# Expert products of a fused attention and mixture-of-experts layer: scaled and summed on VectorE from PSUM, with the clipping of all heads on GpSimd

## What is computed

```python
exp_x = jnp.exp(jnp.clip(x - x_max, -50.0, 50.0))      # first ("plain") attention, all 16 heads
...
h = _swiglu(flat @ W1_shared)                          # one hidden layer shared by the 8 experts
for e in range(E):                                     # E = 8; w is zero except for two experts a token
    routed = routed + h @ W2_experts[e] * w[:, e:e + 1]
out = x + (shared + routed)
return _rmsnorm(out, norm2_w)
```

## Time and profile before

| what | value |
| --- | --- |
| median of 3 runs | 1968.94 us (1968.68 to 1974.44) |
| profiled execution: its time, its span | 1971.31 us, 1969.5 us |
| mean granted TensorE clock | 0.979 of full speed |
| PE busy | 1798.6 us (91%) |
| DVE busy | 1633.5 us (83%) |
| ACT busy | 1446.3 us (73%) |
| POOL busy | 1180.6 us (60%) |

### The profile page before, as it was taken

One profiled execution on the slowest core, in us unless ns is written; L12 is line 12 of the kernel. 1 busy time (PEld: TensorE's weight loads), 2 busy tenths in 40 slices (PEclk: granted clock), 3 DMA queues, 4 the chain that ended last, 5 costly groups with the idle time before them and its releaser, 6 DMA issues.

```text
span 1969.5 us, 33956 instructions
## 1 busy us (share of the span) xinstructions
PE 1798.6 (91%) x10244; PEld 526.8 (27%) x10244; DVE 1633.5 (83%) x2741; ACT 1446.3 (73%) x3095; POOL 1180.6 (60%) x1759
## 2 busy tenths in 40 slices
PE   5888899999999999999999999999999999999964
PEld 1122222222222232222222232222222222222222
DVE  4999998979899898989889898989989898987110
ACT  1378777778787788788777788777778887877622
POOL 3344548466674847567584856657485666738244
PEclk9899999999999999999999999999999999999977
DMA  4122222212122221212222121212222121220100
GB/s 123 31 64 73 72 70 59 76 56 84 57 63 76 60 80 56 84 57 71 70 58 81 57 81 57 82 57 59 81 61 78 56 85 57 62 69 28 45 25 6
DMA packets 120255, 126.34 MB, mean 64 GB/s; under 512 B 35196, under 2 KB 86780, under 8 KB 119932
## 3 DMA queue, kind: packets, MB, share of 16 engines
q1 hardware_dynamic: 119112, 123.39, 21.0%
q10 hardware_dynamic: 960, 0.79, 0.2%
HBM read 29.11 MB, written 22.02 MB: 26 GB/s over the span
## 4 chain that ended last, share of the span: by engine, by line
PE 55%; DVE 27%; SPq 7%; issue 4%; DMA 3%; ACT 3%; POOL 1%; POOLq 0%; ACTq 0%; DVEq 0%
DVE negmax L857 18%; PE score_ps L550 15%; PE o_ps L585 13%; PE side_ps L657 13%; SPq L394 6%; PE side_ps L644 4%; DVE weights L865 2%; PE side_ps L626 2%; PE side_ps L630 2%; PE side_ps L614 1%; DMA res_old<-res_new 1%; PE shift_ps L565 1%; PE side_ps L649 1%; DVE hidden L902 1%; PE side_ps L600 1%
## 5 line engine op out<-in xcount | busy, mean ns | idle before, releaser
L857 DVE TENSOR_REDUCE negmax<-score_ps 128x1 f32<-128x512 f32 x2048 | 1293.5, 681 | 167.5 <-PE score_ps L550 160.2
L693 ACT ACTIVATE weights<-shift_ps 128x512 f32<-128x512 f32 x2048 | 1114.2, 604 | 273.6 <-PE shift_ps L565 249.6
L550 PE MATMUL score_ps<-kt,qt 48*128 48x512 bf16 x2048 | 670.0, 394 | 74.6 <-DVE negmax L857 55.7
L565 PE MATMUL shift_ps<-qt,kt 51*128 51x512 bf16 x2048 | 655.8, 387 | 8.5 <-DMA qt<-max_rows 5.3
L585 PE MATMUL o_ps<-weights,vt 128*32 128x512 f32 x4096 | 551.4, 611 | 0.4 <-POOL weights L1048 0.4
L1048 POOL TENSOR_SCALAR weights<-weights 128x2048 f32<-128x2048 f32 x192 | 366.0, 1906 | 207.6 <-ACT weights L693 189.6
L550 PEld LDWEIGHTS score_ps<-kt,qt 48*128 48x128 bf16 x2048 | 148.7, 94 | 850.0 <-DVE negmax L857 746.8
L657 PE MATMUL side_ps<-w_sb,hidden 128*128 128x512 f32 x512 | 255.7, 622 | 18.6 <-ACT spread L727 14.0
L727 ACT ACTIVATE spread<-side_ps,gate 128x128 f32<-128x128 f32 x512 | 159.5, 372 | 134.2 <-PE side_ps L657 132.4
L644 PE MATMUL side_ps<-x1T,w_up_sb 128*128 128x512 f32 x256 | 151.7, 676 | 16.0 <-DVE hidden L902 8.6
L565 PEld LDWEIGHTS shift_ps<-qt,kt 51*128 51x128 bf16 x2048 | 150.3, 94 | 43.3 <-ACT weights L693 30.8
(11 more groups left out here) (108 smaller groups left out, 1407.5 us busy)
## 6 DMA issues: line engine op xcount, KB each, us to landing
qt<-q_parts SPq DMA_DIRECT2D x768, 32.0 KB
kt<-k_parts SPq DMA_DIRECT2D x744, 32.0 KB
o_rows<-o_sb SPq DMA_DIRECT2D x64, 256.0 KB, 2.0
swung<-turned SPq DMA_DIRECT2D x64, 128.0 KB, 2.4
heads_raw<-o_rows SPq DMA_DIRECT2D x64, 128.0 KB
inv_wide<-inv_rows SPq DMA_DIRECT2D x32, 256.0 KB, 3.3
x_in<-in_x_dram SPq DMA_DIRECT2D x16, 256.0 KB, 3.5
xn_mid<-xn_new SPq DMA_DIRECT2D x16, 256.0 KB, 3.4
```

Of the source, the lines that this page charges most:

```text
L550: pe.matmul(score_ps[:, score_bank(a, t), :], qt[a][row:row + HROWS, slot, 128 * tile:128 * tile + 128], kt[a][row:row + HROWS, slot, :], ...
L565: pe.matmul(shift_ps[:, shift_bank(a, t), :], kt[a][row:row + HROWS + MROWS, slot, 128 * tile:128 * tile + 128], qt[a][row:row + HROWS + M ...
L693: act.activation(weights[:, i % 8, tile, :], shift_ps[:, shift_bank(a, t), :], ACT.Exp, scale=SCALE).then_inc(weighed, 1)
L857: dve.tensor_reduce(negmax[:, i // 8, tile, i % 8:i % 8 + 1], score_ps[:, score_bank(a, t), :], AX.X, ALU.max, negate=True).then_inc(max_t ...
```

## The change

- ACT's `weight_experts` (32 scaled copies of 128 x 128 in an iteration) and POOL's `mix` (24 additions) go, with their three buffers.
- DVE gets a `mix` of its own. In quarter t of exp n and again in quarter t + 1 it does two instructions on 128 x 128 that read a product from PSUM and the gate as a per-row scalar: one multiplies and adds into `out_sb`, the other into a second sum `others` (which the first product of a tile writes with a plain multiplication). The second pair waits on the semaphore of the first and frees the bank.
- POOL's new `join` adds `others` to `out_sb` at the start of the next even step (128 x 512), in front of `square_out`.
- POOL clips all 16 heads; DVE's eight half-head clips go. Head 15 is clipped first thing in the next even step. PE waits for POOL's clip alone.
- POOL's lists are reordered: `root` before the first `rope_less_first`, `finish` behind the first part of `router`, `divide` of the rotary attention between clips 6 and 7 (before: behind clip 8), `third` behind clips 4 and 5.
- Eight entries of AT move: z 28 to 26 (ACT), shares 36 to 34 and square_x1 47 to 45 (DVE), act_v 1 to 0, act_q_plain_2 3 to 4; dve_exp is new, act_exp and act_exp_gap go.

```diff
-      "copy0": 52, "z": 28, "shares": 36, "top": 27, "square_x1": 47,
+      "copy0": 52, "z": 26, "shares": 34, "top": 27, "square_x1": 45,
...
-                        pe.wait_ge(clip_pool, cnt(b, lag, 12, 3 * quad + 3))
-                        pe.wait_ge(clip_dve, cnt(b, lag, 8, 2 * quad + 2))
+                        pe.wait_ge(clip_pool, cnt(b, lag, 16, 4 * quad + 4))
...
+            def mix(b, n, half):
+                if not live(b, -2):
+                    return
+                tile, e = n // 2, 2 * half
+                if half == 0:
+                    full(dve, b, f"exp{n}")
+                    if n == 0:
+                        dve.wait_ge(route, cnt(b, -2, ROUTE_A + ROUTE_B, ROUTE_A + ROUTE_B))
+                        need(dve, joined, cnt(b, -2, 1, 0))
+                        taken(dve, b, "shared_out")
+                    else:
+                        taken(dve, b, f"exp{n - 1}")
+                else:
+                    dve.wait_ge(mixed, cnt(b, -2, 8, n + 1))
...
+                dve.scalar_tensor_tensor(out=out_sb[:, tile, :], in0=product(0), scalar=share_of(0),
+                                         in1=out_sb[:, tile, :], op0=ALU.mult, op1=ALU.add)
+                if n % 2 == 0 and half == 0:
+                    last = dve.tensor_scalar(others[:, tile, :], product(1), share_of(1), None, ALU.mult)
+                else:
+                    last = dve.scalar_tensor_tensor(out=others[:, tile, :], in0=product(1), scalar=share_of(1),
+                                                    in1=others[:, tile, :], op0=ALU.mult, op1=ALU.add)
+                last.then_inc(mixed if half == 0 else free(f"exp{n}"), 1)
...
+            def join(b):
+                if live(b, -3):
+                    taken(pool, b + (-1), "exp7")
+                    pool.tensor_tensor(out_sb[:], out_sb[:], others[:], ALU.add).then_inc(joined, 1)
+                    pool.wait_ge(joined, cnt(b, -3, 1, 1))
...
             def even(b):
+                clip(b + (-1), 15)
                 split_max(b, "max_rope1")
                 square_out(b)
                 turn(b, 0)
                 turn(b, 1)
+                root(b, -3, 1)
                 rope_less_first(b, 0, q_rest, q_parts)
-                root(b, -3, 1)
                 rope_less_first(b, 1, k_rest, k_parts)
+                router(b, True)
                 finish(b)
-                router(b, True)
...
             def square_out(b):
                 if live(b, -3):
+                    join(b)
                     pool.tensor_tensor(square, out_sb[:], out_sb[:], ALU.mult).then_inc(squared, 1)
...
             def odd(b):
                 clip(b, 0)
                 split_max(b, "max_plain1")
                 clip(b, 1)
                 clip(b, 2)
-                mix(b, 0)
+                clip(b, 3)
+                clip(b, 4)
                 third(b, 1, PLAIN, 0, q_rest, q_parts)
+                clip(b, 5)
                 third(b, 1, PLAIN, 1, k_rest, k_parts)
-                mix(b, 1)
...
                 clip(b, 6)
+                divide(b, ROPE)
+                clip(b, 7)
                 clip(b, 8)
-                divide(b, ROPE)
+                clip(b, 9)
                 split_max(b, "max_rope0")
-                mix(b, 5)
                 square_x1(b)
-                clip(b, 9)
+                clip(b, 10)
                 place_v(b, ROPE)
                 root(b, -1, 0)
-                clip(b, 10)
-                mix(b, 6)
+                clip(b, 11)
+                clip(b, 12)
                 norm_weight(b, x1, 0, -1, x1_done)
-                mix(b, 7)
-                clip(b, 12)
                 clip(b, 13)
                 clip(b, 14)
```

## The result

The changed kernel takes **1939.48 us** (median of four runs, 1936.54 to 1945.56) against 1969.36 before: ratio 0.985, 95% interval 0.982 to 0.988. Measured again beside later runs it took 1943.26 (six runs), ratio 0.987, 0.985 to 0.989. The profiled execution is the longest of the first four, 1945.56 us with a span of 1943.7. PE is busy 93% of it, DVE 84%, ACT 68% and POOL 55%.

The account below looks back on a forecast made before the run. PE bounds the odd step's exp0 to exp6, DVE its last 15.60 us. 1971.3 - 25 - 4 - 3 + 2 = 1941.3, less 2.4 for the median: 1939 us; range 1925 to 1964, the forecast's own 1928 to 1948 (chance 0.62).

Parts of the forecast that it names:

- The main term: End of the odd step: DVE loses head 11's half clips, gains exp7's pairs; net 1.8 us a step, 25 in 14.
- What was to be late next: End of odd step: DVE waits some 0.4 us for quarter 54's score, then k_rope reads hold PE about a microsecond.
- The price of a pair: Two new DVE instructions on 128 x 128 from PSUM: 0.28 us alone, 0.48 a pair; upper end 0.74.
- the cover of 0.2: Behind exp0 to exp6: DVE's pair, maximum and pair take 1.66 us of PE's 1.86 other work, leaving 0.2; cost nothing.
- Rival B: New DVE instructions cost ACT's 372 ns, 0.74 a pair; PE loses 1.15 us a step; 1964 us total; chance 0.13.
- rival C: DVE's mixes wait for POOL's clips as its half clips did: 9 us a step, about 2065 us total; chance 0.09.
- The first batches: Batches 0 and 1 have no experts, so clips go without replacement: 4 us gained in batch 0, 0 in batch 1.
- place (1): POOL's odd step: division now before clip 7, which may reach PE late; 0 to 0.6 us a step, 2 in all.
- The end: After the last scores: exps 0.1 us nearer, 1.6 in all, plus about 1 at ACT's scaling of x; together 3.
- the way of x1: At the end, ACT's copies no longer stand before its scaling of x: 0 to 1.1 us gained, say 1.
- Places (2) and (3): POOL's clip 15 and join before the square DVE sums; `finish` and `third` behind the router's step: both costed at 0.
- Rival A: POOL's new order gives half the gain back, 0.6 and 0.4 us a step, 14 in all: 1953 us; chance 0.16.

Follow-up runs that it names:

- Experiment 8: Changed kernel with the division behind clip 8 and exp7's product handled as before (ACT copies, POOL adds behind clip 14): 1945.17 us, ratio 0.988.
- Experiments 1 to 4: Kernel before, POOL clipping all heads: 2029.01 us; changed kernel, DVE half clips kept: 1967.39; kernel before, head 11's clip to POOL: 1980.55; first without POOL's additions: 1944.86.
- experiment 5: Changed kernel with POOL's clip 9 back behind the square of x1 and clip 10 behind the root: 1952.16 us, ratio 0.990.
- experiment 9: Changed kernel with the constant 0.25 in place of the gate's per-row scalar in all 32 scaled sums of a batch: 1931.82 us, ratio 0.980.
- experiment 10: Changed kernel with a third DVE instruction in each pair, writing a product times its gate to an unread tile: 2001.68 us, ratio 1.015.
- Experiment 6: Kernel before with POOL's twelve clips a batch left out, DVE's half clips and POOL's additions kept: 1943.41 us, ratio 0.987.
- experiments 7, 11 and 12: Changed kernel with the division behind clip 8: 1940.00 us; with z, shares, v and q_plain's second part at old quarters: 1940.97; repeated unchanged: 1943.26.
- experiment 3: Kernel before with only head 11's clip moved from DVE to POOL, ahead of its mix 6: 1980.55 us, ratio 1.005.

## Why the prediction was right

**The time and the step that gives it.** 1939 us were predicted and 1939.48 measured. That they agree so closely is luck: the same kernel took 1943.26 in its second measurement, and several smaller terms were wrong, as told below. The main term is not luck. The end of the odd step was to give 1.8 us in each of 14 steps, and gave 1.72 from quarter 47 to 63 in most steps and 1.7 to 1.9 in undisturbed iterations. What was to be late next was late next: 0.30 of DVE for a score where 0.4 was put, then PE at the reads of k_rope, 0.82 and 0.21. PE's idle time in the second part fell from 3.1 to 1.41, where about 1.5 was put. Experiment 8 shows that the waits at k_rope are the limit: with less work for DVE ahead of them, they stay as long.

**What the argument left out.** It priced DVE's side of the exchange and took POOL's room as a matter of order. Experiments 1 to 4 show that it is the condition: in the last 15.60 us of the odd step before, DVE was busy 15.51 and POOL 14.43, and of the second number the prediction made no use. A clip given to POOL comes back as a wait for POOL unless POOL loses its additions; the mixes on DVE bring nothing unless the half clips go. The halves alone are worth +60 and -2 us (the second within the noise), both together -24 to -30. It also missed that clips 9 and 10 get better places (experiment 5).

**The price of a pair.** It took 0.48 from a statistic without a per-row scalar; 0.60 from start to end and 0.52 along the chain were measured, and experiment 9 puts the difference on the scalar. From the cycles in the Trainium skill, "VectorE: DVE Perf Modes", the section on the TRN2 errata, the prediction had estimated 0.52 a pair, and left it; the chain has 0.52. Behind exp0 to exp6 the size mattered little, since 0.09 us of the cover of 0.2 was left. At the end of the odd step and in the tail it did matter: the cheaper pairs of experiment 9 are worth 8 to 11 us in all. Rival B's mechanism is real, though: experiment 10 takes 0.52 more behind each exp and is 60 us slower. B failed on its price, 0.74 a pair: a DVE instruction lasts almost ACT's 372 ns, but the next begins 0.26 us after its start.

**No wait for POOL's clips (rival C).** The spread of 339 to 352 ns in the tile gate, with 156 of the 512 beside a clip, excludes it, while a half clip is 0.68 us alone and 2.05 beside POOL. Experiment 6 removes POOL's clips and most of the stretch. The Trainium skill, "GPSIMD Engine Reference", Specifications, says that VectorE contends with GpSimd in 2-port modes and with two SBUF inputs. The trace agrees for the mixes, which read one SBUF tensor at most and are not stretched. The half clip has one SBUF input too and is stretched, so by the page it would run in a 2-port mode; no run here shows the mode itself.

**The first batches.** -4 was predicted, -0.8 was there at the landmark of batch 2. Batch 0 did end its odd step 4.4 us earlier, but in batch 1 PE lost most of it behind place (1) of POOL's order. POOL's and PE's timelines:

```profile
199.92 1.26 POOL L1129 TENSOR_TENSOR headsT<-heads_raw,inv_wide 128x512 f32<-128x512 f32 x1 [4.04 <-DMA inv_wide<-inv_rows]
201.27 5.84 POOL L1050 TENSOR_SCALAR weights<-weights 128x2048 f32<-128x2048 f32 x3
```

```profile
203.22 1.94 PE L581 MATMUL o_ps<-weights,vt 128*32 128x512 f32 x8 [3.15 <-POOL weights L1050]
```

Clip 7 ends at 203.16. In the steady steps this place cost 0.22 and 0.49 us, once each: 3.8 in all where 2 was put, nearly all of it in one step.

**The end.** -3 was predicted, and -3.4 measured from the last landmark but one on, by other pieces, so the number is luck. The exps were to be 0.1 nearer to each other and are 0.12 further apart (3.33 against 3.21 in the earlier trace rows): two pairs are 1.35 with the gate, and 1.10, as put, with a constant. The gain is the odd step of batch 15, 3.1, which the prediction had in its 14 steps, and the way of x1, 1.4. There ACT's scaling did stand behind the copies of exp7, as put, but exp7 itself ran slowly, at a granted clock of 0.66 from 1890 to 1895. PE's timelines, before and after:

```profile
1890.49 3.65 PE L657 MATMUL side_ps<-w_sb,hidden 128*128 128x512 f32 x4 [0.88 <-DVE x L880]
```

```profile
1865.81 1.98 PE L653 MATMUL side_ps<-w_sb,hidden 128*128 128x512 f32 x4 [0.88 <-DVE x L851]
```

With 1.98 before too, the copies would have ended at about 1893.6 (an estimate: 1890.49 + 1.98 and 1.14 for the copies), ahead of the 1893.85 at which POOL had the norm for that scaling, and this piece would have given nothing.

**Places (2) and (3) of POOL's order** cost nothing, as taken. DVE's sum over the squares has no wait before it until the last scores are through, and clip 15 starts behind 1.18 us of waiting for ACT. SP's store of the earlier trace rows starts 29.0 us after the first score of its even step, where it was 29.25. Rival A stays at the 3.8 us above.

**The sum** over the profiled executions is -25.8 where -30 was put. The first batches gave 3.2 too little, and the end, with the odd step of batch 15 in it, 3.4 where 3 + 1.8 were put. The 13 iterations between gave 21.6, near the 13 x 1.8 less 2 for place (1), but by more pieces than the prediction had. Along PE's scores the ends of the odd steps gave 24.1, and the even steps up to quarter 48 gave 2.7, which was put at nothing. The parts with exp0 to exp6 took back 1.6, and the stretch from quarter 48 of the even step to quarter 8 of the odd one, where PE waits for queries and keys, took back 3.6. Behind two such waits (0.93 at 501.48, 1.09 at 502.96) the granted clock was also down, 0.55 from 505 to 510. The 24.1 is 24.0 to 24.1 in the profiled executions of experiments 7, 11 and 12 as well, while the last piece goes there from -1.9 to +5.0: the gain is steady, and what differs between these executions lies mostly in that piece.

## What to carry to other kernels

When two engines are both full in the same stretch, price a move between them from both sides: what the giving engine gains is lost again unless the taking engine sheds as much in that stretch, and each half tried alone can look like a failure. When covered work is estimated to end a few tenths of a microsecond before it is wanted, that cover is part of the price: what the next instruction added there takes beyond it is paid on every repetition. Take the price of a small instruction from one with the same kinds of operands, per-row scalars included.

## What the runs showed of the hardware

A per-row scalar instead of a constant costs a DVE instruction on 128 x 128 from PSUM 64 ns (345 against 281), and brings two of them from 0.20 to 0.26 us apart.

A late POOL in the last steps can cost far more than its wait. In experiment 3 PE stood 3.48 us for POOL at max_rope1 in the tail, where the kernel before stands 0.15 for ACT. PE's timeline, then two windows (columns as in the earlier trace rows):

```profile
1818.72 0.58 PE L608 MATMUL side_ps<-ident_bf,max_parts 128*24 128x128 bf16 x4 [3.48 <-POOL max_parts L1014]
```

```profile
1820.00:1825.00 5.00, 5.00 (x21) 0.77 (x20) 0.28 (x1) 3.02 (x6) 1.21 (x2) 0.50 0.16 61
1825.00:1830.00 5.00, 5.00 (x16) 2.41 (x12) 0.20 (x1) 1.08 (x2) 0.00 (x0) 0.50 0.00 0
```

The granted clock then stood at 0.50, the lower of its two levels (1.2 GHz), until after 1835, and PE got through 15 to 21 matmuls in 5 us, where the kernel before, at 1.00, has 23 to 32 there. From the last landmark but one to the last it took 103.0 us against 93.5, all of what this kernel lost. Its ten runs spread from 1968.3 to 1984.0, the fastest with a mean granted clock of 0.981 and the slowest with 0.973; whether this stretch makes that spread is open, since one execution has a trace.

The lower clock shows also between the exps of the last batch, where PE has nothing else to do. Windows of the changed kernel, then of experiment 10:

```profile
1910.00:1920.00 10.00, 5.96 (x13) 2.04 (x12) 3.65 (x12) 0.00 (x0) 0.00 (x0) 1.00 0.00 0
```

```profile
1960.00:1970.00 10.00, 5.77 (x8) 1.85 (x8) 3.98 (x14) 0.00 (x0) 0.00 (x0) 0.76 0.00 0
1970.00:1980.00 10.00, 6.35 (x8) 1.84 (x8) 3.39 (x13) 0.00 (x0) 0.00 (x0) 0.66 0.00 0
```

In the changed kernel PE is idle 1.35 us ahead of each exp, and the clock there was at full speed (2.4 GHz). In experiment 10 it is idle 1.86; the clock came from 0.50 (1920 to 1950), and among the exps it rose and fell again, so that four matmuls took between 1.98 and 3.78 us. The idle time alone does not decide it: four exps of the batch before in the same run, from 1893.42 to 1904.96, have the same 1.86 ahead of them and took 1.98 each. From the last square of x1 to the end that is 90.7 us against 77.9, of which the third instructions themselves are 8 x 0.52 = 4.2.
